# Query stage of a Nyström attention and mixture-of-experts layer: norms in four column tiles, a second output tile, gate products in front of the second attention half

## The reference, cut to what matters

```python
landmarks = K[:, :, landmark_idx, :]
Phi_Q = exp(-sq_dists(Q, landmarks) / temperature)     # 64 values per head and token
Phi_K = exp(-sq_dists(K, landmarks) / temperature)
W_kernel = exp(-W_sq / temperature) + REG * eye(64)
Y = solve(W_kernel, einsum('bhnk,bhnd->bhkd', Phi_K, V))
norm = max(einsum('bhnk,bhko->bhno', Phi_Q, solve(W_kernel, sum(Phi_K))), 1e-10)
x = layernorm(x + (Phi_Q @ Y / norm) @ Wo.T + bo)
gate_logits = x @ Wg.T + bg
topk_vals, topk_idx = top_k(gate_logits, 2); gate_w = softmax(topk_vals)
x = layernorm(x + sum over the two experts e of gate_w[e] * (x @ We[e].T + be[e]))
# sq_dists(X, L) = max(|X|^2 + |L|^2 - 2 X L, 0), the |X|^2 per head
```

## Time and profile before

| | |
|---|---|
| median of 3 runs | 2056.58 us (2052.75 to 2057.75) |
| the profiled execution | 2053.05 us, span 2051.3 us |
| query loop, a usual turn | about 42.8 us, 32 turns |
| PE busy in the span | 1835.4 us, 89% |
| DVE busy | 1577.8 us, 77% |
| ACT busy | 1230.0 us, 60% |
| POOL busy | 930.2 us, 45% |
| chain that ended last, by engine | PE 48%, DVE 25%, DMA 10% |

### The profile page before, as it was taken

The page is one execution under the profiler, slowest core; times in us unless marked ns, Lnnn a source line. Parts: engine busy times, 40 slices in busy tenths (PEclk is TensorE's granted clock), DMA queues, the critical chain, the costliest instruction groups (busy, mean ns, idle before and its releaser), DMA issues.

```text
span 2051.3 us, 41908 instructions
## 1 busy us (share of the span) xinstructions
PE 1835.4 (89%) x15928; PEld 1351.7 (66%) x15928; DVE 1577.8 (77%) x3316; ACT 1230.0 (60%) x2411; POOL 930.2 (45%) x1179
## 2 busy tenths in 40 slices
PE   4488999999967999999999999999999999999997
PEld 3177878778753666666666666666666666666665
DVE  5678844997336788888888888888888888888874
ACT  2265666676654475667557666656755756675553
POOL 2300000000002466666666666666666666656666
PEclk9689999999986999999999999999999999999999
DMA  2676687777862333333342334333334333233300
GB/s 82 106 171 147 160 191 166 169 166 184 171 184 65 88 85 85 86 80 83 93 102 74 88 78 100 75 98 85 81 77 103 87 84 92 73 89 87 88 26 21
DMA packets 184637, 213.95 MB, mean 104 GB/s; under 512 B 57692, under 2 KB 108276, under 8 KB 184180
## 3 DMA queue, kind: packets, MB, share of 16 engines
q1 hardware_dynamic: 184244, 210.75, 42.8%
q0 software_dynamic: 192, 0.52, 0.1%
HBM read 61.26 MB, written 23.59 MB: 41 GB/s over the span
## 4 chain that ended last, share of the span: by engine, by line
PE 48%; DVE 25%; DMA 10%; issue 8%; SPq 5%; ACT 2%; POOL 1%; DVEq 0%; POOLq 0%; ACTq 0%
PE bank L298 11%; PE bank L300 10%; PE bank L299 10%; DMA out<-y_out 8%; PE bank L1623 6%; PE bank L1483 2%; PE bank L1593 2%; PE bank L1499 2%; PE bank L1484 2%; DVE inversion L1048 2%; DVE if L1249 2%; DVE phi L1020 2%; DVE y_out L1291 1%; DVE y_out L1290 1%; DVE inversion L1050 1%
## 5 line engine op out<-in xcount | busy, mean ns | idle before, releaser
L298 PE MATMUL bank<-weh,x1h 128*128 128x512 f32 x1024 | 430.7, 421 | 34.3 <-DVE y_out L1291 33.7
L300 PE MATMUL bank<-wel,x1h 128*128 128x512 f32 x1024 | 405.3, 396 | 0.0
L299 PE MATMUL bank<-weh,x1l 128*128 128x512 f32 x1024 | 405.3, 396 | 0.0
L837 ACT ACTIVATE part_x<-bank,gate 128x256 f32<-128x256 f32 x512 | 211.4, 478 | 211.3 <-PE bank L300 207.2
L545 POOL TENSOR_TENSOR x_tok<-x_tok,bo_sb 128x1024 f32<-128x1024 f32 x32 | 76.8, 2400 | 522.9 <-DMA x_tok<-in_x 522.9
L298 PEld LDWEIGHTS bank<-weh,x1h 128*128 128x128 f32 x1024 | 192.7, 188 | 147.7 <-DVE y_out L1291 55.0
L782 ACT ACTIVATE phi<-bank,nlt_cur,invt 128x512 f32<-128x512 f32 x256 | 187.3, 795 | 77.0 <-PE bank L1593 77.0
L637 ACT ACTIVATE phi<-bank,invt 128x512 f32<-128x512 f32 x256 | 162.5, 685 | 102.2 <-PE bank L1484 102.0
L300 PEld LDWEIGHTS bank<-wel,x1h 128*128 128x128 f32 x1024 | 192.9, 188 | 46.3
L299 PEld LDWEIGHTS bank<-weh,x1l 128*128 128x128 f32 x1024 | 193.5, 189 | 33.8
L557 POOL TENSOR_TENSOR part_x<-part_x 128x512 f32<-128x512 f32 x128 | 183.5, 1434 | 8.5 <-ACT part L837 8.5
(11 more groups left out here) (191 smaller groups left out, 4577.7 us busy)
## 6 DMA issues: line engine op xcount, KB each, us to landing
x_raw<-in_xT SPq DMA_DIRECT2D x64, 512.0 KB, 5.6
q_stack<-kh SPq DMA_DIRECT2D x256, 128.0 KB, 2.4
x_tok<-in_x SPq DMA_DIRECT2D x32, 512.0 KB, 4.1
q_stack<-kl SPq DMA_DIRECT2D x128, 128.0 KB, 2.4
q_stack<-augk SPq DMA_DIRECT2D x32, 512.0 KB, 4.5
out<-y_out SPq DMA_DIRECT2D x64, 256.0 KB, 2.6
k_hl<-attn_h SPq DMA_DIRECT2D x32, 256.0 KB
k_ha<-attn_h SPq DMA_DIRECT2D x32, 256.0 KB
```

Of the source, the lines that this page charges most:

```text
L298: nc.tensor.matmul(outp, ah, bh, start=first, stop=False)
L299: nc.tensor.matmul(outp, al, bh, start=False, stop=False)
L300: return nc.tensor.matmul(outp, ah, bl, start=False, stop=last)
L837: last = nc.scalar.activation(parts[t % 2][q - 1][:, u * D:(u + 1) * D], bank[2 + q % 2][:, u * D:(u + 1) * D], ACT.Copy, scale=gate[at][: ...
```

## The change

Three edits in the query stage.

1. The query norms take the form of the key norms: the products of `key_norms` become a function `quarter_norms`, used for both; VectorE splits 128 rows of 128 columns into `key_hi` and `key_aug`; SyncE copies the four quarters by four DMAs.
2. A second output tile `y_spare`. `y_out` is a list of two, used in turn by the parity of the chunk, with a store semaphore for each tile and half, and `combine` of chunk p waits for the store of chunk p - 2. Space comes from `augk0` and `aug_hi`, which are not held through the query stage any more.
3. In TensorE's turn `gate_logits(c)` moves in front of `attention(q, 1)`; in VectorE's turn `norm_begin(q, 1)` moves behind `gates_begin(c)`, and so `finish(p, 1)` and `gates_begin(c)` come ahead of it.

```diff
-        augk = [sb("augk0", [64, CH], f32r)]
-        aug_hi = sb("aug_hi", [32, CH], f32r)
+        with nc.sbuf_tensor("augk0", [64, CH], f32r) as augk0, nc.sbuf_tensor("aug_hi", [32, CH], f32r) as aug_hi:
+            augk = [augk0]
+        y_spare = sb("y_spare", [P, TPC, D])
+        key_hi, key_aug = sb("key_hi", [P, P], f32r), sb("key_aug", [P, P], f32r)
...
-        x_tok, y_out = sb("x_tok", [P, TPC, D]), sb("y_out", [P, TPC, D])
+        x_tok, y_out = sb("x_tok", [P, TPC, D]), [sb("y_out", [P, TPC, D]), y_spare]
...
-                sp.dma_start(raw(q_stack[96:128]), rep(raw(augk[0][0:32, :]), 1, PAIRS)).then_inc(q_stacked, 16)
+                for t in range(TPC):
+                    sp.dma_start(raw(q_stack[96:128, :, t * P:(t + 1) * P]),
+                                 rep(raw(key_aug[32 * t:32 * t + 32, :]), 1, PAIRS)).then_inc(q_stacked, 16)
...
-                                     y_out[:, 2 * half:2 * half + 2]).then_inc(res_stored, 16)
+                                     y_out[p % 2][:, 2 * half:2 * half + 2]).then_inc(res_stored[p % 2][half], 16)
...
                 dve.wait_ge(qnorm_done, c + 1)
-                norm_rows(augk[0][0:32, :], bank[6]).then_inc(qaug_done, 1)
+                own.then(V.tensor_copy(key_hi[:], bank[6][:, 0:P]))
+                V.scalar_tensor_tensor(key_aug[:], raw(key_hi[:]), lo_sign, bank[6][:, 0:P], ALU.mult,
+                                       ALU.add).then_inc(qaug_done, 1)
...
-                dve.wait_ge(res_stored, 32 * p + 16 * (t // 2) + 16)
-                a = y_out[:, t]
+                if p >= 2:
+                    dve.wait_ge(res_stored[p % 2][t // 2], 16 * (p // 2))
+                a = y_out[p % 2][:, t]
...
-                    norm_begin(q, 1)
                     finish(p, 1)
                     gates_begin(c)
+                    norm_begin(q, 1)
                     combine(p, 3, me)
...
+            def quarter_norms(dst):
+
+                for s in range(KC):
+                    for t in range(TPC):
+                        last = mm(dst[32 * t:32 * t + 32, 0:P], neg_block[:, s, :], sq[:, s, t * P:(t + 1) * P],
+                                  start=(s == 0), stop=(s == KC - 1))
+                return last
...
-                square_norms(bank[6]).then_inc(qnorm_done, 1)
+                quarter_norms(bank[6]).then_inc(qnorm_done, 1)
...
                     experts(p, 10, me)
+                    gate_logits(c, nxt)
                     attention(q, 1)
-                    gate_logits(c, nxt)
                     experts(p, 11, me)
```

More of the change, by code:

```diff
@@ L153, in program @@
             l_hh, l_lo = [[sb1(f"l_{n}0", [P, GROUPS, 4, NL], f32r)] for n in ("hh", "lo")]
-            key_hi, key_aug = sb1("key_hi", [P, P], f32r), sb1("key_aug", [P, P], f32r)
             with ExitStack() as setup:
@@ L182, in program @@
         winv_sb, y_cur = sb("winv_sb", [64, H, NL]), sb("y_cur", [P, PAIRS, 64])
-        we_raw = [a[:].rearrange("p t d -> p (t d)") for a in (*x1, y_out, part)]
+        we_raw = [a[:].rearrange("p t d -> p (t d)") for a in (*x1, y_out[0], part)]
         idx_loaded, small_loaded, w_loaded, we_loaded = (sem("idx_loaded"), sem("small_loaded"), sem("w_loaded"),
@@ L228, in program @@
             sem("ffn_done"), sem("comb_done"), sem("part_ready"), sem("part_sum"), sem("acc_done"), sem("ln2_stats"), sem("ln2_coef"),
-            sem("res_ready"), sem("res_stored"))
+            sem("res_ready"), [[sem(f"res_stored{i}{half}") for half in range(2)] for i in range(2)])
         block = ctx.enter_context(nc.Block())
@@ L290, in groups_of @@
             return a[:].rearrange("p (s j) n -> p j s n", s=KC)[:, j]
-        STACKED = 16 * 13
+        STACKED = 16 * 16
         KH_STACKED, AUG_STACKED = 16 * 6, 16 * TPC
@@ L313, in _ @@
             sp.sem_inc(zt_saved, 1)
-            sp.sem_inc(res_stored, 32)
             sp.sem_inc(xqh_ready, 2)
@@ L484, in _ @@
             turn(BATCH - 1)
-            sp.wait_ge(res_stored, 32 * (NCH + 1))
+            for i in range(2):
+                for half in range(2):
+                    sp.wait_ge(res_stored[i][half], 16 * NCH // 2)
         @block.gpsimd
@@ L843, in result @@
                 act.wait_ge(ln2_coef, TPC * p + t + 1)
-                nc.scalar.activation(y_out[:, t], y_out[:, t], ACT.Identity, bias=nm2[:, t:t + 1],
+                y = y_out[p % 2]
+                nc.scalar.activation(y[:, t], y[:, t], ACT.Identity, bias=nm2[:, t:t + 1],
                                      scale=rs2[:, t:t + 1]).then_inc(res_ready, 1)
@@ L1296, in finish @@
                 dve.wait_ge(comb_done, TPC * p + t + 2)
-                V.tensor_tensor(y_out[:, t], y_out[:, t], parts[t % 2][0][:, 0:D], ALU.add).then_inc(acc_done, 1)
+                y = y_out[p % 2]
+                V.tensor_tensor(y[:, t], y[:, t], parts[t % 2][0][:, 0:D], ALU.add).then_inc(acc_done, 1)
                 dve.wait_ge(acc_done, TPC * p + t + 3)
-                own.then(V.bn_stats(st2[:, t], y_out[:, t]))
+                own.then(V.bn_stats(st2[:, t], y[:, t]))
                 dve.sem_inc(dve_waited, 1)
@@ L1462, in key_norms @@
                     pe.wait_ge(prod_read, done[-1])
[L1463 to L1467, removed]
+                quarter_norms(bank[4]).then_inc(norm_done, 1)
             def dists(c, t):
```

## The result

The changed kernel takes 2028.5 us (median of 4 runs, 2024.3 to 2032.6) beside 2057.2 us for the kernel before (2052.8 to 2059.8): ratio 0.9863, 95% interval 0.9835 to 0.9890, so 22 to 34 us less. The forecast was 2032 us, 24 us less. Beside later kernels the changed one was timed twice more, with ratios 0.9838 and 0.9824.

A forecast was written before the change was run, and what follows sets the result against it. Each query turn was taken as a VectorE-bound half plus a TensorE-bound half. Terms -14.6 - 7 - 2 = -23.6 us gave 2029.5 from the profiled execution, 2033 from the median; forecast 2032 us, range 2022 to 2042.

The forecast's parts named there:

- Half one is VectorE's, half two TensorE's: Query turn: first attention half's end to gate transposes (22.29 us) bound by VectorE; transposes to that end (20.51 us) by TensorE.
- Second output tile, -14.6 us: VectorE's combination of token tile 0 no longer waits for the previous chunk's store; TensorE's wait goes wholly, -14.6 us.
- Norms on TensorE, 0 by itself: Query norm block falls from 1.90 to 0.62 us, but TensorE then waits 1.28 us longer for VectorE's combination: 0.
- rival D: Norm saving comes through if VectorE's half-one stalls fall away: -37 us more, 1995 us; sign, wait below 1 us; chance 0.13.
- the first gate part keeps its place beside GpSimd: VectorE's long operations in the first gate part keep their place relative to GpSimd, so no stall is saved there.
- Norm copies, -7 us: Four DMAs into q_stack, the last landing 4.7 us after first issue; TensorE's 9.9 us wait nearly goes, -7 us.
- The moved gate products, -2 us: Reordered gate products and VectorE calls in half one: -2 us over the run, between -4 and +15.
- The walk: VectorE's new order in half one: combination 0.46 us later, second gate part's stalls 0.60 us less, g_st 0.14 us earlier.
- The margin of 0.2 us for the low part of x1: Moved gate products start at 1230.65; VectorE ends the low part of x1 by 1230.44, 0.2 us of margin.
- the sum of the forecast: Whole run: -14.6 - 7 - 2 = -23.6 us; forecast 2032 us, 24 us less.

The follow-up runs named there:

- norms_only: The norm edit alone (products, VectorE's split, four copies) on the kernel before: 2036.9 against 2053.2 us, ratio 0.9924.
- order_only: The two moved calls alone, old norms and one output tile, on the kernel before: 2047.5 against 2053.2 us, ratio 0.9972.
- tile_norms: The changed kernel without the two moved calls: 2026.0 us, ratio 0.9870 to the kernel before.
- norm_late: The changed kernel with norm_begin(q, 1) moved further, behind query_norms: 2056.9 us, ratio 0.9989 to the kernel before.
- norms_x4: The changed kernel with the query stage's norm products done four times over: 2020.5 us, ratio 0.9809 to the kernel before.
- gates_first_x4: The changed kernel with gates_begin(c) ahead of finish(p, 1) and norm products done four times: 2020.3 us, ratio 0.9817 to the kernel before.
- gates_first: The changed kernel with gates_begin(c) ahead of finish(p, 1) on VectorE: 2046.0 us, ratio 0.9949 to the kernel before.

## Why the prediction was right, point by point

- **Half one is VectorE's, half two TensorE's.** Shown, by norms_only (TensorE work taken away in half one: 0.03 us of it arrives) and by the two runs with work added there. The cut between the halves is not sharp in the changed kernel: three of the four turns with half one at 20.7 us follow a half two of 20.6 us, and the fourth one of 20.3, so that what a late half two costs comes back behind it.
- **Second output tile, -14.6 us.** The wait is gone as forecast. As a part of its own it could not be tried beside the old norms, since both do not fit in the memory. On top of the norm edit it is worth about 11 us (0.9924 to 0.9870), on top of norms and order about 8 to 16 us (0.9901 to the three ratios of the change).
- **Norms on TensorE, 0 by itself.** Right as a term: the block is 1.25 us shorter, and in norms_only next to nothing of it arrives. The wait grew from 0.45 to 2.08 us (2.2 forecast), but only in 11 of the 29 turns. In the others it is under 0.8 us: TensorE has waited for ScalarE's `part` already, or runs at the lower clock, or VectorE is early, and the rest of the slack shows as a wait for `g_st` of up to 1.4 us. The sign for rival D (a wait below 1 us) was so met in most turns, and in 4 usual ones its mechanism too: VectorE's stalls of half one fell away. The prediction's sentence that the first gate part keeps its place beside GpSimd did not hold: `oh` ran without a stall in 15 of the 22.
- **Norm copies, -7 us.** The parts are issued over 2.57 us and land after 2.5 us each (2.9 taken from the key stage). SyncE's row of one turn, and the row of the DMA issues, both of the changed kernel:

```profile
1155.29 2.57 SPq L434 DMA_DIRECT2D q_stack<-key_aug  x4
```

```profile
q_stack<-key_aug SPq DMA_DIRECT2D x128, 128.0 KB, 2.5
```

  The wait fell by 7.7 us, to 2.2 us in 6 places ("at most 0.2 us" a turn was forecast, and it is up to 0.8 where it comes). But the norm edit alone brought 16 us. The term was mis-sized in three ways. First, it left out that the store moves forward with the copies, above. Second, an idle time in a row is less than the stall costs. From the transposes to the distances TensorE took 5.95 us with 0.29 us idle, and takes 5.51 without; to the third expert product 10.05 us with 0.79 us idle in the two places, and 8.83 without. The stalls cost 1.22 us where the rows say 0.79. The rows count idle from the modelled end of a matmul, and in a running chain the next starts before that end. Third, against the term: where a copy is still late, half two is 1.4 us longer for 0.2 to 0.9 us of wait, as shown above.
- **The moved gate products, -2 us.** The walk gave half one 0.14 us less; it is 0.22 less (22.25 to 22.03), and order_only confirms it with 3 to 8 us. In the change itself the clock takes part of this back. Both stalls of the second gate part are gone in 11 of the 22 usual turns: in 7 as the walk had it, and in 4 with a stall of `oh` gone as well. In the other 11 they stay or grow, and a stall of `oh` has gone instead, which the walk did not have. So the term came out, and in half of the turns by another way than forecast; that is luck. In order_only half one is 22.0 us in either form. The margin of 0.2 us for the low part of x1 was missed: TensorE waits for it 14 times, 5.2 us in sum, the row at 1183.54.
- **Left out: TensorE's clock.** The forecast left the granted clock as it was. In the loop of before it never falls. After the change it does, in the changed kernel's windows of 2 us (columns as above):

```profile
1062.00:1064.00 2.00, 1.74 (x14) 1.05 (x6) 1.97 (x4) 0.22 (x1) 1.84 (x3) 1.00 0.92 210
1064.00:1066.00 2.00, 0.18 (x1) 0.18 (x2) 1.93 (x5) 0.61 (x2) 0.58 (x1) 0.96 0.19 43
1066.00:1068.00 2.00, 2.00 (x5) 1.61 (x6) 1.76 (x11) 0.00 (x0) 0.00 (x0) 0.50 0.00 0
```

  The matmuls on either side of the wait of 2.08 us in it:

```profile
1063.11 0.39 PE L300 MATMUL bank<-weh,x1l 128*128 128x512 f32 x1
1063.34 0.40 PE L301 MATMUL bank<-wel,x1h 128*128 128x512 f32 x1
1065.82 0.79 PE L299 MATMUL bank<-weh,x1h 128*128 128x512 f32 x1 [2.08 <-DVE y_out L1299]
1066.41 0.63 PE L300 MATMUL bank<-weh,x1l 128*128 128x512 f32 x1
1066.84 0.63 PE L301 MATMUL bank<-wel,x1h 128*128 128x512 f32 x1
```

  The clock is at full before and while TensorE stands, and at 0.50 behind it: starts are 0.23 us apart before the wait (1063.11, 1063.34) and 0.43 after (1066.41, 1066.84). There are 12 such stretches, 20 us of full-clock work. Still a usual turn is no longer than in tile_norms with its one stretch (41.63 against 41.79 us), so part of the 20 us must fall into time in which TensorE would have waited anyway. Turn by turn the trace bears this out. Six stretches begin in the second attention half, behind the moved gate products, ahead of that wait. Four of their turns have a half one of 22.40 to 22.47 us, where turns of the same kind with no stretch have 22.03 to 22.44: 0.4 us each at the most. The other six begin within 1.2 us behind a wait of 2.08 or 2.5 us, and there the time counts: half one is 23.50 us with 1.35 us lost, the next half two 20.57 instead of 19.2 with 1.47 us lost. By this the 12 cost some 10 to 12 us, an estimate (six at 1.7 us and six at 0 to 0.4). So the sum of the forecast, 24 us against 28 measured, comes out by errors that offset each other: the stalls were dearer than their rows, the clock and the late copies took time back. That it is so close is in part luck.

What sets off a stretch stays open in part. My first theory, the wait of 2.08 us, covers the turns shown, but in the changed kernel only half of the stretches begin behind such a wait. It doesn't cover norm_late, norms_x4 and gates_first_x4 either, where no wait of a usual turn is that long. All kernels with more than two stretches have the gate products moved *and* the norms in column tiles; with the old order there is at most one, and order_only has two. That stretches cost time is shown by gates_first; which mix of gaps brings them is not.

## What to carry to other kernels

Cut a turn of a pipelined loop at the points where one engine is released by the other, and ask for each stretch whose chain it is; an edit is worth only what it takes from the owner's chain, and the rest reappears as a wait (here 0.45 to 2.08 us). Price a stall of TensorE by differences between starts of matmuls with and without it, not by the idle time in its row. And when an edit leaves TensorE idle in gaps, look at the granted clock: cheap work in a gap costs nothing here and, as in gates_first, may give back more than it takes. And hold several turns side by side, not one: with GpSimd in a slightly different place the same kernel stalls at another operation.

## What the runs showed of the hardware

- The lower clock level costs the same each time: 1.71 us of full-clock time per stretch, or just double that, in every kernel that has one. A kernel whose TensorE is busy for 1157 of 1220 us still had 12 of them.
- Four DMAs of 128 KB in runs of 512 bytes took no longer than one of 512 KB in runs of 2 KB: first issue to last landing 1.9 + 2.5 = 4.4 us against 4.5 us.
- VectorE's stalls beside GpSimd last until GpSimd's instruction ends, whichever part they meet: `if` ended 0.9 us late in the change, `gs`, `gw` and `oh` 0.8, 1.0 and 0.5 us late in gates_first, where `gs` ends at 1099.39 and GpSimd's operation at 1099.36, `gw` at 1100.76 and GpSimd's at 1100.74.
- Either engine can be the one that is slowed. In the usual turn at 815 us VectorE's clamps of `phi` take 0.81 us each and GpSimd's sum beside them (line 561, at 831.34) 1.86 us; in the turn with late norm copies the clamps take 1.77, 1.78 and 1.22 us and the same operation 1.30 us. That the overlap with GpSimd is the cause there is inferred, not tested.
